# Four PSUM banks instead of two, and a row maximum taken in eight pieces, in the first FFN product of both layers

## The chip, the cores and the metric

The kernel runs on the 8 cores of one Trainium2 chip. Every core runs the same program on one of the 8 batch elements, a 4096 x 1024 float32 array, with its own copy of all weights; the cores exchange nothing. The metric is the device time of the slowest core in microseconds (us). The median of three runs of the kernel before is 11104.93 us.

Each core has five engines that run side by side and wait for each other by semaphores: TensorE (PE in the profile; its weight loads have a row of their own, PEld), VectorE (DVE), ScalarE (ACT), GpSimd (POOL, unused but for constants) and SyncE (SP), which issues all DMAs here.

## The reference

Two layers, each an attention block and an FFN block, each block wrapped in layer norms and a residual. Cut to the part that matters, for one core (`x` is 4096 x 1024):

```
x = x + LN(attn0(LN(x)));   x = x + LN(ffn0(LN(x)))     # layer 0
x = x + LN(attn1(LN(x)));   x = x + LN(ffn1(LN(x)))     # layer 1

act_quant(h):  s = 127 / max(max|h| over the row, 1e-5);  q = clip(round(h*s), -128, 127)
weight_quant:  w -> -1, 0 or 1, with one scale for the whole matrix
ffn:  h = gelu( act_quant(x) @ w1q.T * scales (+ b1 in layer 0) )    # 4096 x 4096
      y = act_quant(h) @ w2q.T * scales (+ b2 in layer 0)
```

Layer 0's FFN has a second layer norm with gamma and beta in front of it and biases b1 and b2; layer 1's has none of these. The quantized numbers are small integers and are held exactly in bf16.

## The kernel before

The kernel is written engine by engine: a function emits a piece of each engine's instruction list, with semaphore waits by hand. Each engine runs its own list strictly in the order in which it was emitted. There is no scheduler. The phases (attention 0, FFN 0, attention 1, FFN 1) are separated by barriers over all engines, and each FFN phase has two halves: the first (product with w1, GELU, quantization, result stored to HBM as `h_q`) and the second (product with w2, layer norm, residual). The change is in the first half, in the function `ffn`.

The first half loops over 32 tiles of 128 rows. For a tile `tt` there are three pieces:

- `front(tt)`: SP loads the rows (`xa`); DVE and ACT take the layer norm's statistics (in layer 0 two norms in a row), DVE the row maximum (L1298) and the scale, ACT scales and rounds (L1352, L1356), DVE clips to bf16 (`xq`, L1316), PE transposes (L181) into `psT`, and DVE copies that to `xqT` (L1322).
- `back_a(tt)`: PE multiplies `xqT` with the 1024 x 4096 weights in eight column groups k of 512; a group is 8 accumulating matmuls (L1395) into one 512-column bank of the PSUM tile `psS` (2048 columns in all). Before, group k uses bank k % 2. In layer 0, DVE scales the group and adds the bias into `ha` (`epi k`, L1411), which frees the bank, and ACT takes the GELU into `hbuf` (`gel k`, L1440). In layer 1, ACT takes the GELU straight from the bank with the scale (`gel k`, L1449), and that frees it. A semaphore mark kept in `ffn1_rel` makes group k wait for the bank's last reader. After `gel7`, DVE takes the maximum of |hbuf| over all 4096 columns in one instruction (L1420), then the scale in four tiny ones (L1423 to L1430) and an empty instruction (L1433) that signals `qn2`; ACT then scales `hbuf` by it (`t2`, L1455; in layer 0 also L1460).
- `back_b(tt)`: DVE clips to bf16 (`hq`; L1479 in layer 0, L1484 and L1488 in layer 1; the mark is `clp2`), and SP stores it.

The loop emits, for k = 0 to 32: `front(k+1)`, `back_b(k-1)`, `back_a(k)`. So on PE the transposes of tile k+1 stand ahead of the groups of tile k, and on DVE everything of `front(k+1)` and the clip of tile k-1 stand ahead of the row maximum of tile k. In layer 1, `gel0` of a tile also waits until the clip of the tile before has read `hbuf` (`hbfree`). The names in the rows drop buffer numbers: `fam` is the row maximum and also, from the change on, its eight partial ones `fam8`; `fst`, `frsc`, `fsact` are [128,1] scales and statistics.

Of the kernel before, what the change touches and what calls it, by code (L numbers as in the profile page):

```python
# [6 lines left out]
F32 = mybir.dt.float32  # L7
BF16 = mybir.dt.bfloat16
AF = mybir.ActivationFunctionType
ALU = mybir.AluOpType  # L10
AX = mybir.AxisListType
# [15 lines left out]
class MK:  # L27
    def __init__(self, phases=("l0a", "l0f", "l1a", "l1f"), debug=False):
# [13 lines left out]
        d = {}  # L42
# [30 lines left out]
        def sb(name, shape, dt, stack=None):  # L73
            return (stack or self._stack).enter_context(nc.sbuf_tensor(name, shape, dt))
# [37 lines left out]
        self.ftmp = sb("ftmp", [128, 32], F32)  # L112
        self.rden = sb("rden", [128, 4], F32)
        self.rden8 = sb("rden8", [128, 8], F32)
        self.am = sb("am", [128, 1], F32)
        self.sact = sb("sact", [128, 1], F32)
        self.rsc1 = sb("rsc1", [128, 1], F32)
# [1053 lines left out]
    def ffn(self, L):  # L1171
        me, blk, d = self, self.block, self.d
# [4 lines left out]
        with contextlib.ExitStack() as ph:  # L1177
            wq1T = self.sb("wq1T%d" % L, [128, 8 * HID], BF16, ph)
            ha = self.sb("ha%d" % L, [128, 4096], F32, ph)
            hb = self.sb("hbuf%d" % L, [128, 4096], F32, ph)  # L1180
# [16 lines left out]
                    self.replicate_vec("bet0", erep, 1024)  # L1197
                self.barrier()

            ffn1_rel = [None, None]  # L1200
            carry = {"xa": [None, None], "trq_prev": None, "gel7_prev": None,
                     "hqst": None}
            plans = {}
# [3 lines left out]
            def seg_marks(P, eng, items):  # L1207
                base = max(me.cnt[eng], _plan[eng])
                mm = {k: base + i + 1 for i, k in enumerate(items)}
                _plan[eng] = base + len(items)  # L1210
                key = {"v": "vm", "s": "sm", "t": "tm"}[eng]
                P.setdefault(key, {}).update(mm)
                return mm

            def buf(tt):
                p = tt % 2
                return dict(
                    lnap=lna[:, p * 1024:p * 1024 + 1024],
                    ln2p=lna[:, 2048:3072],
                    lnxp=lnx[:, 0:1024],  # L1220
                    xqp=xq[:, 0:1024],
                    xqTp=xqT[:, p * 1024:p * 1024 + 1024],
                    st6p=me.fst6[:, p * 12:p * 12 + 12],
                    st2p=me.fst2[:, p * 2:p * 2 + 2],
                    rstdp=me.frstd[:, p:p + 1],
                    nbp=me.fnb[:, p:p + 1],
                    lntp=me.flnt[:, p:p + 1],
                    amp=me.fam[:, p:p + 1],
                    sc1p=me.fsact[:, p * 2:p * 2 + 1],
                    sc2p=me.fsact[:, p * 2 + 1:p * 2 + 2],  # L1230
                    rscp=me.frsc[:, p:p + 1],
                    xap=me.xa[:, p * 1024:p * 1024 + 1024])
# [140 lines left out]
            def back_a(tt):  # L1373
                P, B = plans[tt], buf(tt)
                seg_marks(P, "t", ["mm%d" % k for k in range(8)])
                va = []
                if L == 0:
                    va += ["epi%d" % k for k in range(8)]
                va += ["qn2"]
                seg_marks(P, "v", va)  # L1380
                seg_marks(P, "s", ["gel%d" % k for k in range(8)] +
                          (["t2", "rnd2"] if L == 0 else ["t2"]))
                vm, sm, tm = P["vm"], P["sm"], P["tm"]

                @blk.tensor
                def _(t):
                    for k in range(8):
                        hf = k % 2
                        t.wait_ge(me.semh["v"], vm["evq"])
                        if ffn1_rel[hf] is not None:  # L1390
                            sem, val = ffn1_rel[hf]
                            me.w(t, sem, val)
                        last = None
                        for dc in range(8):
                            last = t.matmul(  # L1395
                                me.psS[:, hf * 512:hf * 512 + 512],
                                B["xqTp"][:, dc * 128:dc * 128 + 128],
                                wq1T[:, dc * HID + k * 512:dc * HID + k * 512 + 512],
                                start=(dc == 0), stop=(dc == 7))
                        assert me.mark(last, "t") == tm["mm%d" % k]  # L1400
                        ffn1_rel[hf] = ("v", vm["epi%d" % k]) if L == 0 else \
                                       ("s", sm["gel%d" % k])

                @blk.vector
                def _(v):
                    if L == 0:
                        for k in range(8):
                            v.wait_ge(me.semh["t"], tm["mm%d" % k])
                            if k == 0 and carry["gel7_prev"] is not None:
                                v.wait_ge(me.semh["s"], carry["gel7_prev"])  # L1410
                            iv = v.scalar_tensor_tensor(  # L1411
                                out=ha[:, k * 512:k * 512 + 512],
                                in0=me.psS[:, (k % 2) * 512:(k % 2) * 512 + 512],
                                scalar=B["rscp"],
                                in1=brep[:, k * 512:k * 512 + 512],
                                op0=ALU.mult, op1=ALU.add)
                            assert me.mark(iv, "v") == vm["epi%d" % k]
                    v.wait_ge(me.semh["s"], sm["gel7"])
                    v.drain()
                    v.tensor_reduce(out=B["amp"], in_=hb[:], axis=AX.X, op=ALU.max,  # L1420
                                    apply_absolute_value=True)
                    v.drain()
                    v.tensor_scalar(out=B["amp"], in0=B["amp"], scalar1=EPS,  # L1423
                                    scalar2=None, op0=ALU.max)
                    v.drain()
                    v.reciprocal(out=B["sc2p"], in_=B["amp"])
                    v.drain()
                    v.tensor_scalar(out=B["sc2p"], in0=B["sc2p"], scalar1=127.0,
                                    scalar2=None, op0=ALU.mult)
                    v.tensor_scalar(out=me.rs2all[:, tt:tt + 1], in0=B["amp"],  # L1430
                                    scalar1=1.0 / 127.0, scalar2=None, op0=ALU.mult)
                    v.drain()
                    assert me.mark(v.nop(), "v") == vm["qn2"]  # L1433

                @blk.scalar
                def _(s):
                    for k in range(8):
                        if L == 0:
                            s.wait_ge(me.semh["v"], vm["epi%d" % k])
                            iv = s.activation(out=hb[:, k * 512:k * 512 + 512],  # L1440
                                              in_=ha[:, k * 512:k * 512 + 512],
                                              func=AF.Gelu)
                        else:
                            s.wait_ge(me.semh["t"], tm["mm%d" % k])
                            if k == 0:
                                s.wait_ge(me.semh["v"], vm["qnt"])
                                if carry.get("hbfree") is not None:
                                    s.wait_ge(me.semh["v"], carry["hbfree"])
                            iv = s.activation(  # L1449
                                out=hb[:, k * 512:k * 512 + 512],  # L1450
                                in_=me.psS[:, (k % 2) * 512:(k % 2) * 512 + 512],
                                func=AF.Gelu, bias=0.0, scale=B["rscp"])
                        assert me.mark(iv, "s") == sm["gel%d" % k]
                    s.wait_ge(me.semh["v"], vm["qn2"])
                    iv = s.activation(out=hb[:], in_=hb[:], func=AF.Identity,  # L1455
                                      bias=me.magic[:], scale=B["sc2p"])
                    assert me.mark(iv, "s") == sm["t2"]
                    if L == 0:
                        s.drain()
                        iv = s.activation(out=hb[:], in_=hb[:], func=AF.Identity,  # L1460
                                          bias=me.nmagic[:], scale=1.0)
                        assert me.mark(iv, "s") == sm["rnd2"]
                carry["gel7_prev"] = sm["gel7"]
# [408 lines left out]
```

## Time and profile before

| what | value |
|---|---|
| median of 3 runs | 11104.93 us (11089.94 to 11122.39) |
| profiled execution | 11115.35 us |
| its span on the slowest core, core 2 | 11113.8 us (fastest core 11079.0) |
| PE / DVE / ACT busy, share of the span | 46% / 40% / 28% |
| DMA queue, share of 16 engines | 13.9% |

No engine is busy for half of the span, so the share of busy time does not say what bounds the kernel; the chain that ended last does. It goes through PE, DVE and ACT by turns (38%, 26% and 18% of the span). A busy PE is not PE at its peak: the granted clock of TensorE (mean 0.70 here) stands in the profile as a share of its full 2.4 GHz, and 0.50 is its lower level, 1.2 GHz.

### The profile page before, as it was taken

How to read it: one execution, taken by the hardware profiler on the slowest of the kernel's cores; microseconds unless marked ns; L12 is line 12 of the kernel's file. 1: busy time of each engine (PE TensorE's matmuls, PEld its weight loads, DVE VectorE, ACT ScalarE, POOL GpSimd, SP SyncE). 2: the span in 40 equal slices, each digit the busy share in tenths (PEclk: the TensorE clock that was granted, in tenths of full speed). 3: DMA queues.
4: the chain of work that ended last, by engine and by line, in shares of the span. 5: the costliest groups of instructions: out<-in, count | busy, mean ns of one | idle time of the engine just before them, and what ended most of it. 6: DMA issues, size and time to landing. Idle time of an engine off the chain costs nothing.

```text
span 11113.8 us, 84236 instructions; the slowest of 8 cores (11079.0 to 11113.8 us)
## 1 busy us (share of the span) xinstructions
PE 5084.5 (46%) x24204; PEld 2302.6 (21%) x24204; DVE 4472.0 (40%) x9414; ACT 3124.4 (28%) x3876; POOL 1.0 (0%) x7
## 2 busy tenths in 40 slices
PE   3445765133333256633333444545544344443666
PEld 1112322111111133311111112212221111111333
DVE  2222333444444432223345555555555433334222
ACT  1111223334444321102223333332332433332111
POOL 0000000000000000000000000000000000000000
PEclk9787777566666668866666666666666577775888
DMA  2111011401111222220000000000001211114222
GB/s 72 42 34 56 29 38 54 146 23 34 34 34 34 98 99 76 76 78 27 27 19 16 16 12 12 8 12 8 8 8 57 89 40 40 40 38 151 76 75 69
DMA packets 159393, 530.32 MB, mean 48 GB/s; under 512 B 49316, under 2 KB 65764, under 8 KB 137447
## 3 DMA queue, kind: packets, MB, share of 16 engines
q1 hardware_dynamic: 158952, 524.93, 13.9%
q8 instruction: 217, 3.56, 0.1%
q14 instruction: 224, 1.84, 0.1%
HBM read 373.88 MB, written 150.99 MB: 47 GB/s over the span
## 4 chain that ended last, share of the span: by engine, by line
PE 38%; DVE 26%; ACT 18%; issue 8%; DMA 4%; DVEq 4%; ACTq 3%; SPq 0%; POOL 0%; POOLq 0%
PE psO L1595 9%; PE psS L1395 8%; PE psT L181 5%; DVE negmh L496 4%; ACT pp L524 4%; PE psS L461 3%; PE psO L1103 3%; PE psO L826 3%; DVE fam L1420 3%; PE psS L654 2%; ACTq L1330 2%; DVE pp L584 2%; DMA wtmp<-w 2%; ACT hbuf L1455 2%; ACT L390 1%
## 5 line engine op out<-in xcount | busy, mean ns | idle before, releaser
L1395 PE MATMUL psS<-wq1T,xqT 128*128 128x512 bf16 x4096 | 1061.7, 426 | 115.4 <-ACT hbuf L1449 100.9
L1595 PE MATMUL psO<-wq2T,hqT 128*128 128x512 bf16 x4096 | 1005.9, 411 | 67.1 <-DVE hqT L1580 67.1
L390 ACT ACT_TABLE_LOAD x128 | 164.2, 1283 | 2891.8 <-DVE st L373 2891.8
L181 PE MATMUL psT<-identb,pp 128*128 128x128 bf16 x4752 | 551.4, 254 | 824.8 <-DVE pp L584 824.4
L496 DVE TENSOR_REDUCE negmh<-psS 128x1 f32<-128x1024 f32 (+5 forms) x720 | 730.1, 1035 | 392.4 <-PE psS L461 369.2
L461 PE MATMUL psS<-kl,qTb 128*128 128x512 bf16 (+3 forms) x1152 | 491.8, 523 | 797.6 <-ACT pp L524 780.1
L524 ACT ACTIVATE pp<-psS,negmh 128x1024 bf16<-128x1024 f32 (+5 forms) x720 | 693.1, 964 | 493.2 <-DVE negmh L496 489.0
L181 PE MATMUL psT<-identb,xq 128*128 128x128 bf16 x512 | 64.7, 307 | 1577.9 <-DVE xq L1316 1577.9
L181 PEld LDWEIGHTS psT<-identb,pp 128*128 128x128 bf16 x4752 | 387.4, 114 | 1054.1 <-issue 935.4
L1395 PEld LDWEIGHTS psS<-wq1T,xqT 128*128 128x128 bf16 x4096 | 440.0, 109 | 712.9 <-issue 343.9
L1121 DVE COPY ppT<-psT 128x512 bf16<-128x512 bf16 x1056 | 443.2, 424 | 347.9 <-PE psT L181 325.1
L1595 PEld LDWEIGHTS psO<-wq2T,hqT 128*128 128x128 bf16 x4096 | 422.9, 104 | 635.5 <-issue 231.7
L1103 PE MATMUL psO<-ppT,vl 128*128 128x512 bf16 x1056 | 463.8, 440 | 196.3 <-DVE ppT L1121 181.0
L1420 DVE TENSOR_REDUCE fam<-hbuf 128x1 f32<-128x4096 f32 x64 | 282.9, 4420 | 507.7 <-ACT hbuf L1449 479.4
L301 ACT ACT_TABLE_LOAD x64 | 82.1, 1283 | 1255.6 <-DVE st L296 1117.2
L181 PE MATMUL psT<-identb,hqs 128*128 128x128 bf16 x2048 | 188.4, 266 | 530.6 <-DVE hqT L1580 515.8
L1610 DVE TENSOR_TENSOR rsc<-rs2all,swv 128x1 f32<-128x1 f32 x64 | 10.2, 160 | 1041.7 <-PE psO L1595 1009.2
L524 ACT ACT_TABLE_LOAD x96 | 123.2, 1283 | 986.9 <-DVE negmh L496 986.9
L181 PE MATMUL psT<-identb,lnb 128*128 128x128 bf16 x512 | 64.8, 307 | 720.0 <-ACT lnb L320 720.0
L181 PEld LDWEIGHTS psT<-identb,xq 128*128 128x128 bf16 x512 | 49.6, 138 | 1608.0 <-issue 1608.0
L461 PE MATMUL psS<-kT,qt 128*128 128x512 bf16 (+3 forms) x1152 | 286.3, 414 | 129.9 <-DVE pp L508 96.9
L1455 ACT ACTIVATE hbuf<-hbuf,magic,fsact 128x4096 f32<-128x4096 f32 x64 | 243.2, 3800 | 355.5 <-DVEq L1433 355.5
(162 smaller groups left out, 7177.6 us busy)
## 6 DMA issues: line engine op xcount, KB each, us to landing
wtmp<-w SPq DMA_DIRECT2D x128, 512.0 KB, 4.2
h_q<-hq SPq DMA_DIRECT2D x64, 1024.0 KB, 4.8
wtmp<-w SPq DMA_DIRECT2D x32, 2048.0 KB, 8.3
hqs<-h_q SPq DMA_DIRECT2D x64, 1024.0 KB, 6.7
xres<-xst SPq DMA_DIRECT2D x96, 512.0 KB, 2.9
xa<-xres SPq DMA_DIRECT2D x96, 512.0 KB, 5.6
xst<-xres SPq DMA_DIRECT2D x96, 512.0 KB, 3.2
xa<-x SPq DMA_DIRECT2D x32, 512.0 KB, 3.6
```

Source lines behind the costliest of these rows:

```text
L181: return te.matmul(out_ap, in_ap, self.identb[:], is_transpose=True, start=start, stop=stop, skip_group_check=True)
L390: s.activation(out=me.lnt[:], in_=me.st2[:, 1:2], func=AF.Ln, bias=me.epsv[:], scale=1.0)
L461: last = t.matmul(ten[:, off + sub:off + sub + sw], qap(dc), kT_ap(dc, CW * c + sub, CW * c + sub + sw), start=(dc == 0), stop=(dc == nchu ...
L496: iv = v.reduce_max(out=me.negmh[:, r * nb + c:r * nb + c + 1], in_=ten[:, off:off + wdt], axis=AX.X, negate=True)
L524: iv = s.activation(out=pp_row[:, CW * c:CW * c + wdt], in_=ten[:, off:off + wdt], func=AF.Exp, bias=me.negmh[:, r * nb + c:r * nb + c + 1 ...
L826: last = t.matmul(me.psO[:, e * 512:e * 512 + 512], ppT[:, ph2 * 512 + jj * 128: ph2 * 512 + jj * 128 + 128], vres[:, jabs * 1024 + e * 51 ...
L1103: iv = t.matmul(me.psO[:, g * 512:g * 512 + 512], vl1[:, (g * NT + j) * 128: (g * NT + j) * 128 + 128], ppT[:, ph2 * 512:ph2 * 512 + 512], ...
L1121: iv = v.tensor_copy(out=ppT[:, ph2 * 512:ph2 * 512 + 512], in_=me.psT[:, ph2 * 1024:ph2 * 1024 + 512])
L1395: last = t.matmul(me.psS[:, hf * 512:hf * 512 + 512], B["xqTp"][:, dc * 128:dc * 128 + 128], wq1T[:, dc * HID + k * 512:dc * HID + k * 512 ...
L1420: v.tensor_reduce(out=B["amp"], in_=hb[:], axis=AX.X, op=ALU.max, apply_absolute_value=True)
L1455: iv = s.activation(out=hb[:], in_=hb[:], func=AF.Identity, bias=me.magic[:], scale=B["sc2p"])
L1595: last = t.matmul(me.psO[:, e * 512:e * 512 + 512], hqT[:, p * 4096 + hc * 128:p * 4096 + hc * 128 + 128], wq2T[:, hc * 1024 + e * 512:hc ...
```

## The change

In `back_a` the eight column groups rotate through four banks of `psS` (k % 4) where they rotated through two, and `ffn1_rel` keeps four marks. The one maximum over 4096 columns becomes eight over 512 columns, each waiting for its own GELU, into the columns of a new [128, 8] tile `fam8`, and a ninth over these eight. The row scale `rs2all` is computed after the drain that stood behind it, and carries the mark `qn2` itself; the empty instruction goes.

```diff
-            ffn1_rel = [None, None]
+            ffn1_rel = [None, None, None, None]
...
-                        hf = k % 2
+                        hf = k % 4
...
-                                in0=me.psS[:, (k % 2) * 512:(k % 2) * 512 + 512],
+                                in0=me.psS[:, (k % 4) * 512:(k % 4) * 512 + 512],
...
-                    v.wait_ge(me.semh["s"], sm["gel7"])
+                    for k in range(8):
+                        v.wait_ge(me.semh["s"], sm["gel%d" % k])
+                        if k == 0:
+                            v.drain()
+                        v.tensor_reduce(out=me.fam8[:, k:k + 1],
+                                        in_=hb[:, k * 512:k * 512 + 512],
+                                        axis=AX.X, op=ALU.max,
+                                        apply_absolute_value=True)
                     v.drain()
-                    v.tensor_reduce(out=B["amp"], in_=hb[:], axis=AX.X, op=ALU.max,
-                                    apply_absolute_value=True)
+                    v.tensor_reduce(out=B["amp"], in_=me.fam8[:], axis=AX.X,
+                                    op=ALU.max, apply_absolute_value=True)
...
-                    v.tensor_scalar(out=me.rs2all[:, tt:tt + 1], in0=B["amp"],
-                                    scalar1=1.0 / 127.0, scalar2=None, op0=ALU.mult)
                     v.drain()
-                    assert me.mark(v.nop(), "v") == vm["qn2"]
+                    iv = v.tensor_scalar(out=me.rs2all[:, tt:tt + 1], in0=B["amp"],
+                                         scalar1=1.0 / 127.0, scalar2=None,
+                                         op0=ALU.mult)
+                    assert me.mark(iv, "v") == vm["qn2"]
...
-                                in_=me.psS[:, (k % 2) * 512:(k % 2) * 512 + 512],
+                                in_=me.psS[:, (k % 4) * 512:(k % 4) * 512 + 512],
```

DVE's list in a middle tile of layer 1 before, from the clip of the tile ahead to the statistics of the tile behind:

```order
L1484 TENSOR_SCALAR hbuf1<-hbuf1,magic 128x4096 [waits s,ev0]
L1488 TENSOR_SCALAR hq1<-hbuf1 128x4096
L1404 UNCONDITIONAL_BRANCH
L1420 TENSOR_REDUCE fam<-hbuf1 128x1 [waits s]
L1423 TENSOR_SCALAR fam<-fam 128x1
L1426 RECIPROCAL fsact<-fam 128x1
L1428 TENSOR_SCALAR fsact<-fsact 128x1
L1430 TENSOR_SCALAR rs2all<-fam 128x1
L1433 NO_OP
L1263 UNCONDITIONAL_BRANCH
L1267 BN_STATS fst6<-xa 128x6 [waits xa0]
```

The same place in the changed kernel, whose lines have moved by one to nine:

```order
L1493 TENSOR_SCALAR hbuf1<-hbuf1,magic 128x4096 [waits s,ev0]
L1497 TENSOR_SCALAR hq1<-hbuf1 128x4096
L1405 UNCONDITIONAL_BRANCH
L1423 TENSOR_REDUCE fam8<-hbuf1 128x1 [waits s] x8
L1428 TENSOR_REDUCE fam<-fam8 128x1
L1431 TENSOR_SCALAR fam<-fam 128x1
L1434 RECIPROCAL fsact<-fam 128x1
L1436 TENSOR_SCALAR fsact<-fsact 128x1
L1439 TENSOR_SCALAR rs2all<-fam 128x1
L1264 UNCONDITIONAL_BRANCH
L1268 BN_STATS fst6<-xa 128x6 [waits xa0]
```

One waiting reduction has become eight that wait (`x8`) and one that does not; the empty instruction is gone. What stands ahead and behind is the same. On PE and ACT the lists keep their instructions and their order; only the banks and the values waited for change.

## Rows read from the trace of the kernel before

**Rows 1.** The page: chain that ended last, shares by engine and line.
```profile
PE psO L1595 9%; PE psS L1395 8%; PE psT L181 5%; DVE negmh L496 4%; ACT pp L524 4%; PE psS L461 3%; PE psO L1103 3%; PE psO L826 3%; DVE fam L1420 3%; PE psS L654 2%; ACTq L1330 2%; DVE pp L584 2%; DMA wtmp<-w 2%; ACT hbuf L1455 2%; ACT L390 1%
```

**Rows 2.** The same chain in 9390 to 9440 us, layer 1, by line.
```profile
by line: PE psS L1395 26.2%; DVE fam L1420 17.7%; ACTq L1330 13.7%; issue 8.0%; ACT hbuf L1455 6.4%; DVE hbuf L1484 4.7%; DVE hq L1488 4.6%; ACT hbuf L1449 4.2%; ACT lna L1335 2.5%; ACT lnx L1352 2.5%; DVE fam L1298 2.4%; ACT lnx L1356 2.3%
```

**Rows 3.** Groups, layer 0 (2300 to 3800): busy us, mean ns | idle before, releaser.
```profile
L1395 PE MATMUL psS<-wq1T,xqT 128*128 128x512 bf16 x2048 | 519.7, 421 | 14.5 <-DVE ha L1411 14.5
...
L1420 DVE TENSOR_REDUCE fam<-hbuf 128x1 f32<-128x4096 f32 x32 | 141.4, 4420 | 28.3 <-ACT hbuf L1440 28.3
```

**Rows 4.** The same groups in layer 1 (8770 to 10040).
```profile
L1395 PE MATMUL psS<-wq1T,xqT 128*128 128x512 bf16 x2048 | 542.0, 431 | 100.9 <-ACT hbuf L1449 100.9
...
L1420 DVE TENSOR_REDUCE fam<-hbuf 128x1 f32<-128x4096 f32 x32 | 141.4, 4420 | 479.4 <-ACT hbuf L1449 479.4
```

**Rows 5.** Timeline of one tile, layer 1: start, duration, what [idle before].
```profile
9396.69 0.15 DVE L1428 TENSOR_SCALAR fsact<-fsact 128x1 f32<-128x1 f32 x1
...
9397.08 3.80 ACT L1455 ACTIVATE hbuf<-hbuf,magic,fsact 128x4096 f32<-128x4096 f32 x1 [5.50 <-DVEq L1433]
...
9411.01 4.62 PE L1395 MATMUL psS<-wq1T,xqT 128*128 128x512 bf16 x16
...
9417.45 0.32 SPq L1257 DMA_DIRECT2D xa<-xres  x1
9418.27 1.27 ACT L1449 ACTIVATE hbuf<-psS,frsc 128x512 f32<-128x512 f32 x2
...
9419.10 12.21 PE L1395 MATMUL psS<-wq1T,xqT 128*128 128x512 bf16 x48 [3.48 <-ACT hbuf L1449]
...
9429.68 0.69 ACT L1449 ACTIVATE hbuf<-psS,frsc 128x512 f32<-128x512 f32 x1 [1.04 <-PE psS L1395]
9431.41 0.69 ACT L1449 ACTIVATE hbuf<-psS,frsc 128x512 f32<-128x512 f32 x1 [1.04 <-PE psS L1395]
9432.25 4.42 DVE L1420 TENSOR_REDUCE fam<-hbuf 128x1 f32<-128x4096 f32 x1 [15.35 <-ACT hbuf L1449]
```

**Rows 6.** Stretches of that tile, line L1395: PE and PEld busy, PEclk.
```profile
9411.00:9413.00 2.00, 1.99 (x5) 0.77 (x6) 0.50 0.00 0
...
9416.00:9419.00 3.00, 0.00 (x0) 0.00 (x0) 1.00 0.42 175
9419.20:9422.00 2.80, 2.80 (x9) 1.05 (x9) 0.62 0.93 272
```

**Rows 7.** Timeline of PE, another tile of layer 1.
```profile
8889.27 6.06 PE L1395 MATMUL psS<-wq1T,xqT 128*128 128x512 bf16 x16
8897.37 12.21 PE L1395 MATMUL psS<-wq1T,xqT 128*128 128x512 bf16 x48 [2.04 <-ACT hbuf L1449]
```

**Rows 8.** Timeline of PE, the last tile of layer 1.
```profile
10015.10 13.22 PE L1395 MATMUL psS<-wq1T,xqT 128*128 128x512 bf16 x48 [13.79 <-ACT hbuf L1449]
```

**Rows 9.** Timeline of one tile, layer 0: two statistics, then the row maximum.
```profile
2905.55 0.69 DVE L1267 BATCH_NORM_STATS2 fst<-xa 128x6 f32<-128x512 f32 x1 [0.29 <-issue]
2906.16 0.68 DVE L1268 BATCH_NORM_STATS2 fst<-xa 128x6 f32<-128x512 f32 x1
...
2946.21 0.75 DVE L1411 SCALAR_TENSOR_TENSOR ha<-psS,frsc,brep 128x512 f32<-128x512 f32 x1 [0.97 <-PE psS L1395]
2947.06 0.63 ACT L1440 ACTIVATE hbuf<-ha 128x512 f32<-128x512 f32 x1 [1.09 <-DVE ha L1411]
2947.84 4.42 DVE L1420 TENSOR_REDUCE fam<-hbuf 128x1 f32<-128x4096 f32 x1 [0.88 <-ACT hbuf L1440]
2952.34 0.15 DVE L1423 TENSOR_SCALAR fam<-fam 128x1 f32<-128x1 f32 x1
```

**Rows 10.** Groups of DVE, all phases: the small reductions.
```profile
L496 DVE TENSOR_REDUCE negmh<-psS 128x1 f32<-128x512 f32 x36 | 24.9, 691 | 9.8 <-PE psS L461 7.4
...
L537 DVE TENSOR_REDUCE negM<-negmh 128x1 f32<-128x4 f32 x72 | 6.8, 150 | 18.7 <-ACT pp L524 17.4 <-DVE pp L508 1.3
```

**Rows 11.** The load of the FFN's rows (L1257): issue to landing.
```profile
DMA to landing us min/median/max: 3.1/5.6/6.4
```

More of the change, by code:

```diff
@@ L114, in __init__ @@
         self.rden8 = sb("rden8", [128, 8], F32)
+        self.fam8 = sb("fam8", [128, 8], F32)
         self.am = sb("am", [128, 1], F32)
```

## The prediction

> **What bounds the kernel now.** I read the chain of waits first, since no engine is busy for half of the span. Over the whole program the first FFN product (L1395) has 8% of it and the row maximum behind the GELU (L1420) 3% [rows 1]. Cut out for one stretch of layer 1's first FFN half the picture is sharper: the product has 26.2%, the maximum 17.7%, and the rest is a single thread that changes engine at each step [rows 2]. So in layer 1 nothing overlaps the chain: what is cut from a link comes off the end.
>
> Next, the groups by stage. In layer 0 PE runs its 2048 matmuls in 519.7 us and waits only 14.5 us, in one piece; DVE waits 28.3 us in 32 pieces, 0.88 us each, ahead of its maximum. In layer 1 PE is busy 542.0 us and waits another 100.9 us for the GELU's banks, and DVE sits idle 479.4 us ahead of the maximum, about 15 us a tile [rows 3, 4].
>
> The timeline of one tile shows why [rows 5]. PE starts at 9411.01, fills two banks in 4.62 us and stops. The first GELU can start only at 9418.27, behind the clip of the tile before. It frees a bank, and PE goes on at 9419.10, 8.09 us after its start; in a tile whose first two groups took 6.06 us it was 8.10 [rows 7]. Six groups take 12.21 us more, the last GELU starts at 9431.41 and the 4.42 us maximum at 9432.25. The clock shows what the stop costs beyond itself: 0.50 at the start of the stream, 1.00 in the stop, and 0.62 in the first 2.8 us behind it [rows 6], so that PE pays for two slow starts. At 1.00 a group takes 1.73 us (the distance of the last two GELUs, which each wait for PE [rows 5]), or 0.216 us a matmul; at 0.50 twice that.
>
> **The change part by part.**
>
> *A, the tail of the maximum, layer 1.* Before, the large reduction starts 0.84 us after the last GELU starts, and the next DVE instruction follows 4.50 us later (2947.84 to 2952.34 [rows 9]). After, seven of the eight pieces fit in the time in which DVE was idle: GELUs come 0.63 us apart at the tightest (1.27 us for two) and 1.73 us apart towards the end [rows 5]. Only the last piece is behind the last GELU. A 512-column reduction takes 0.69 us and one of 4 columns 0.15 us [rows 10]; the first was from PSUM, but statistics over 512 columns of SBUF also take 0.69 [rows 9]. With 0.08 us from an end to a dependent start (2952.26 to 2952.34 [rows 9]) that is 0.69 + 0.08 + 0.15 + 0.08 = 1.00 us. Gain 3.50 us a tile.
>
> *B, the row scale before the signal, both layers.* Before, the scale's instruction at 9396.69 and ACT's start at 9397.08 are 0.39 us apart, with `rs2all` nearly beside the former [rows 5]. After, it comes behind it: 0.15 + 0.08 + 0.14, then 0.10 us from a marked DVE end to ACT's start (2946.96 to 2947.06 [rows 9]), 0.47 us. Loss 0.08 us a tile. ACT waits for exactly this, so nothing hides it. A and B together: 3.42 x 32 tiles = 109.4 us off layer 1.
>
> *C, four banks, layer 1.* Before, the stream takes busy plus wait: 542.0 + 100.9 = 642.9 us. The last tile has no transposes in front of it and a stream of its own, 13.79 + 13.22 us and 3.5 us of two groups at full clock [rows 8], 30.5 us. The other 31 take 612.4 / 31 = 19.75 us each. After, the third and fourth groups run in the old stop. The fifth needs the first GELU's bank, free at 8.09 us as before. How long the first four take hangs on when the clock rises. The mean stop of the other 31 tiles is (100.9 - 13.79) / 31 = 2.8 us, so their first two groups take 8.09 - 2.8 = 5.2 to 5.3 us; four take 5.2 + 2 x 1.73 = 8.7 us, beyond 8.09, so that the bank is free. The whole stream is 5.2 + 6 x 1.73 = 15.6 us. Gain 19.75 - 15.6 = 4.15 us a tile, x 31 = 128.7 us. Bounds: where the first two groups take 4.62 us [rows 5], the fifth starts at about 8.09 and the stream is 8.1 + 4 x 1.73 = 15.0 us, gain 147 us; where they take 6.06 us [rows 7] it is 16.4 us, gain 103 us. Layer 0's unbroken streams average 519.7 / 32 = 16.2 us [rows 3], inside these bounds. I take the middle, because layer 1's own first groups give it.
>
> *D, the last tile of each half.* There PE waits long with two groups done (13.79 us [rows 8], 14.5 us in layer 0 [rows 3]). With four done, two groups leave the end: 2 x 1.73 = 3.5 us in each layer, 7.0 us.
>
> *E, the pieces in layer 0.* Here all eight pieces stand behind the last bias instruction on DVE, so none of them is hidden behind another engine's work except the last GELU's 0.88 us wait. The last bias instruction ends at 2946.96; a drained start follows 0.09 later; the pieces follow each other as two independent statistics of the same size do, 0.61 us from start to start [rows 9]: 0.09 + 7 x 0.61 + 0.69 + 0.08 + 0.15 + 0.08 = 5.36 us to the next tiny instruction, against 5.38 before. With B's 0.08 that is 0.06 us x 32 = 1.9 us lost. Bounds: nothing to gain below that pace; at most each piece pays its 0.69 us and a fresh 0.15 us wait (9432.10 to 9432.25 [rows 5]), 0.84 apart: 7 x 0.23 = 1.6 us a tile more, 54 us in all. I take the low end, since only the pair is the same case: independent, same engine, nothing late. The banks do nothing in layer 0: PE never waited for one except in D.
>
> The Trainium skill (VectorE: DVE Perf Modes, section The DRAIN you can't avoid) says that after a Vector instruction "the next op does not start until the 8-stage pipe empties". By that the pieces would be 0.69 apart, layer 0 would lose 18 us more and the sum would come to 10880; the trace does not agree, as the second statistic starts 0.08 us before the first ends.
>
> *Covers.* The new rows' load is issued at 9417.45 and lands at most 6.4 us later [rows 11], 9423.9. Their statistics move from behind 9432.25 + 5 us to about 9429.5, so 5 us of cover are left. PE's idle time between streams shrinks by the tail's 3.4 us; I give nothing for a warmer start, as a 13.79 us wait did not keep the clock up either (48 matmuls in 13.22 us where full clock needs 10.4 [rows 8]).
>
> *Sum.* -109.4 (A, B) - 128.7 (C) - 7.0 (D) + 1.9 (E) = -243.2 us on 11115.35, the profiled execution: 10872. The median of the runs is 10.4 us lower; the same cut on it gives 10862. The other cores, at most 35 us shorter, run the same chain.
>
> **The rivals.**
>
> *1. The pieces cost their full price in layer 0.* For it: eight waits and eight starts a tile on DVE's path. Against: the pair 0.61 apart. Price 54 instead of 1.9 us: -191, 10914.
>
> *2. The stream gains nothing.* The clock could fall again in mid-stream as it does now, or PE could stop at the fifth group for as long as now at the third. For it: the fifth still waits for the same GELU. Against: four groups outlast 8.09 us on average. Then only A, B and E count: -107.5, 10997.
>
> *3. Slower: the clock never rises in layer 1's stream.* If writing four banks by turns kept the granted clock at 0.50 throughout, a stream takes 64 x 0.432 = 27.6 us, 7.9 more than now, x 31 = 245, against 107.5 gained: +137, 11242. The point from which it decides is a stream longer than 19.75 + 3.4 = 23.2 us. Against: layer 0's unbroken streams take 16.2 us [rows 3], so the clock rises in them, with the same matmuls and a bank change every group.
>
> The Trainium skill (TensorE: Matmul & The Clock Gate, section A second HAM failure mode: psum-queue depth-cycling) describes matmuls of this size that cycle through PSUM banks and idle briefly between groups until the clock swings between its levels. By it the outcome would lie between rivals 2 and 3; layer 0's rows, which also change bank each group, speak against it.
>
> *4. It does nothing that can be measured*, because a wait I have not seen (the load, the store of `hq`) takes the place of the stop: 11105. Against: the 5 us of cover above.
>
> **How the numbers follow.** Forecast 0.80, rival 1 0.09, rival 2 0.06, rival 3 0.03, rival 4 0.02. The bounds of C put the forecast's own range at 10843 to 10888, and run to run the kernel before spreads over 32 us. Rival 1 has 0.09, so I reach just past it: 10838 to 10916. A measurement of this kernel tells about 0.3% (33 us) from no change; the forecast and rivals 1 and 2 lie beyond that: faster 0.95, same 0.02, slower 0.03.
>
> **What would show it.** In layer 1: PE's wait for the GELU down from 100.9 to some 10 us, all but a few in the last tile; streams of 15 to 16.4 us; the last piece starting 0.84 us behind the last GELU and the next tiny instruction 1.00 us behind that; tiles about 7.6 us closer together. In layer 0: pieces 0.61 us apart and tiles as far apart as before. I am wrong if PE stops at the fifth group for more than a microsecond in most tiles, if the clock is at 0.50 for over a third of a stream, or if the pieces start 0.7 us or more apart.

## The result and the profile after

The changed kernel takes 10873.73 us, median of 8 runs, against 11115.45 us of the kernel before, 8 runs beside it: ratio 0.9784, 95% interval 0.9769 to 0.9799. That is 241.7 us less; 243.2 were forecast. The profiled execution took 10869.97 us with a span of 10867.6 on its slowest core, core 7.

The two groups of layer 1 that answer to [rows 4], and the small reduction (columns: busy us, mean ns | idle before, releaser):

```profile
L1396 PE MATMUL psS<-wq1T,xqT 128*128 128x512 bf16 x2048 | 499.7, 408 | 7.7 <-ACT hbuf L1458 6.9
...
L1423 DVE TENSOR_REDUCE fam<-hbuf 128x1 f32<-128x512 f32 x256 | 167.9, 683 | 200.5 <-ACT hbuf L1458 200.1 <-issue 0.2
...
L1428 DVE TENSOR_REDUCE fam<-fam 128x1 f32<-128x8 f32 x32 | 5.2, 161 | 2.4
```

PE's wait for a bank is down from 100.9 to 6.9 us, and that is one piece, in the last tile. Its busy time is down as well, by 42 us with the same 2048 matmuls: the second slow starts are gone. DVE's waits are now between the pieces, where the GELUs set the pace. In layer 0 the stream is what it was in [rows 3], but for the wait in the last tile (11.4 us for 14.5):

```profile
L1396 PE MATMUL psS<-wq1T,xqT 128*128 128x512 bf16 x2048 | 519.4, 421 | 11.4 <-DVE ha L1412 11.4
```

A tile of layer 1, the counterpart of [rows 5] (timeline: start, duration, what [idle before]):

```profile
9523.66 15.16 PE L1396 MATMUL psS<-wq1T,xqT 128*128 128x512 bf16 x64
...
9530.10 0.32 SPq L1258 DMA_DIRECT2D xa<-xres  x1
9530.93 2.43 ACT L1458 ACTIVATE hbuf<-psS,frsc 128x512 f32<-128x512 f32 x4
9531.77 2.46 DVE L1423 TENSOR_REDUCE fam<-hbuf 128x1 f32<-128x512 f32 x4 [2.21 <-ACT hbuf L1458]
...
9538.92 0.69 ACT L1458 ACTIVATE hbuf<-psS,frsc 128x512 f32<-128x512 f32 x1 [1.04 <-PE psS L1396]
9539.72 0.69 DVE L1423 TENSOR_REDUCE fam<-hbuf 128x1 f32<-128x512 f32 x1 [1.04 <-ACT hbuf L1458]
9540.48 0.16 DVE L1428 TENSOR_REDUCE fam<-fam 128x1 f32<-128x8 f32 x1
9540.72 0.15 DVE L1431 TENSOR_SCALAR fam<-fam 128x1 f32<-128x1 f32 x1
...
9541.41 0.15 DVE L1439 TENSOR_SCALAR rs2all<-fam 128x1 f32<-128x1 f32 x1
9541.66 0.69 DVE L1268 BATCH_NORM_STATS2 fst<-xa 128x6 f32<-128x512 f32 x1
9541.66 3.80 ACT L1464 ACTIVATE hbuf<-hbuf,magic,fsact 128x4096 f32<-128x4096 f32 x1 [2.05 <-DVE rs2all L1439]
```

The 64 matmuls are one unbroken row. The first GELU still starts 7.27 us behind the stream's start, as in [rows 5], but by then four groups are done and four GELUs run in a row. The last piece starts 0.80 us behind the last GELU, and the next tiny instruction 1.00 us behind that. The load issued at 9530.10 has 11.6 us until its statistics.

The clock in the same tile (stretch; PE and PEld busy; PEclk) rises once and stays. So it does in 30 of layer 1's tiles on each of the 8 cores (the last two follow each other without a break): it rises 1.5 to 5.2 us into the stream and falls in none.

```profile
9523.00:9525.00 2.00, 1.34 (x4) 0.60 (x5) 0.50 0.03 8
9526.00:9530.00 4.00, 4.00 (x20) 1.82 (x19) 1.00 0.00 0
9530.00:9538.60 8.60, 8.57 (x40) 3.65 (x38) 1.00 0.53 183
```

The end of a tile of layer 0, beside [rows 9]:

```profile
2970.26 0.75 DVE L1412 SCALAR_TENSOR_TENSOR ha<-psS,frsc,brep 128x512 f32<-128x512 f32 x1 [0.97 <-PE psS L1396]
2971.11 4.84 DVE L1423 TENSOR_REDUCE fam<-hbuf 128x1 f32<-128x512 f32 x8
2976.02 0.16 DVE L1428 TENSOR_REDUCE fam<-fam 128x1 f32<-128x8 f32 x1
2976.25 0.15 DVE L1431 TENSOR_SCALAR fam<-fam 128x1 f32<-128x1 f32 x1
```

Eight pieces with a wait each take 4.84 us, and the next tiny instruction starts 5.24 us behind the end of the last bias instruction (2971.01), against 5.38 before. Nothing is gained that matters, and nothing lost: layer 0's tiles are 47.7 to 47.8 us apart, as before, while layer 1's went from 40.0 us to 32.6.

### The profile page after: what moved, and what is told of

Its sections match the earlier page's. It is cut to its first block, busy times and chain, and to the rows that moved or that the text cites. A ratio compares the mean times of both kernels' runs of the same rounds, so it can differ in the third digit from the quotient of the medians.

```text
span 10867.6 us, 85192 instructions; the slowest of 8 cores (10829.9 to 10867.6 us)
## 1 busy us (share of the span) xinstructions
PE 5024.7 (46%) x24204; PEld 2281.8 (21%) x24204; DVE 4528.6 (42%) x9926; ACT 3124.1 (29%) x3876; POOL 1.0 (0%) x7
## 4 chain that ended last, share of the span: by engine, by line
PE 39%; DVE 24%; ACT 17%; issue 8%; DVEq 4%; DMA 4%; ACTq 3%; SPq 0%; POOL 0%; POOLq 0%
PE psO L1604 9%; PE psS L1396 9%; PE psT L182 5%; DVE negmh L497 4%; ACT pp L525 4%; PE psS L462 3%; PE psO L1104 3%; PE psO L827 3%; PE psS L655 2%; ACTq L1331 2%; DVE pp L585 2%; DMA wtmp<-w 2%; ACT hbuf L1464 2%; DVE ppT L1122 2%; ACT L391 1%
## 5 line engine op out<-in xcount | busy, mean ns | idle before, releaser
L1604 PE MATMUL psO<-wq2T,hqT 128*128 128x512 bf16 x4096 | 1028.8, 418 | 67.5 <-DVE hqT L1589 67.5
L1396 PE MATMUL psS<-wq1T,xqT 128*128 128x512 bf16 x4096 | 1019.1, 415 | 19.0 <-DVE ha L1412 11.4
L1423 DVE TENSOR_REDUCE fam<-hbuf 128x1 f32<-128x512 f32 x512 | 322.7, 680 | 203.4 <-ACT hbuf L1458 200.1
L462 PEld LDWEIGHTS psS<-kl,qTb 128*128 128x128 bf16 x1152 | 89.8, 103 | 1184.2 <-issue 1162.5
```

The costliest lines, as they stand in the source:

```text
L462: last = t.matmul(ten[:, off + sub:off + sub + sw], qap(dc), kT_ap(dc, CW * c + sub, CW * c + sub + sw), start=(dc == 0), stop=(dc == nchu ...
L1396: last = t.matmul(me.psS[:, hf * 512:hf * 512 + 512], B["xqTp"][:, dc * 128:dc * 128 + 128], wq1T[:, dc * HID + k * 512:dc * HID + k * 512 ...
L1423: v.tensor_reduce(out=me.fam8[:, k:k + 1], in_=hb[:, k * 512:k * 512 + 512], axis=AX.X, op=ALU.max, apply_absolute_value=True)
L1604: last = t.matmul(me.psO[:, e * 512:e * 512 + 512], hqT[:, p * 4096 + hc * 128:p * 4096 + hc * 128 + 128], wq2T[:, hc * 1024 + e * 512:hc ...
```

## The experiments

The theory: layer 1's chain loses the stop with the slow start behind it (C), and seven eighths of the maximum (A); the two add up, and layer 0 is left alone. Rivals: the parts need each other; a stop costs what it does because of the clock, whatever its length; the pieces cost layer 0 their price.

**Banks alone.** The kernel before with `k % 4` and four marks, nothing else.

> The kernel before with the four banks alone; the one large maximum and the old signal stay. Theory (the banks are worth what the product's stream loses in its stop and its second slow start, terms C and D): layer 1's streams 15.5 to 15.7 us on average, PE's wait for the GELU in layer 1 down from 100.9 to about 10 us, 136 us off the kernel before. Rival (the stream is shortened only together with the pieces, since the maximum sets when the next tile starts and with that when the clock rises): anything from 110 to 154 us, with streams of 15.0 or of 16.4 us in nearly every tile. Second rival (the stop moves to the fifth group): under 30 us.

Ratio 0.9877 (0.9832 to 0.9923), 137 us off, 86 to 187 by the interval, so the time alone decides nothing between the theory and the first rival. Layer 1 on core 1:

```profile
L1395 PE MATMUL psS<-wq1T,xqT 128*128 128x512 bf16 x2048 | 502.6, 410 | 11.1 <-ACT hbuf L1449 10.7
...
L1420 DVE TENSOR_REDUCE fam<-hbuf 128x1 f32<-128x4096 f32 x32 | 141.4, 4420 | 350.3 <-ACT hbuf L1449 350.3
```

The whole of C is there without the pieces: 513.7 us busy and waiting, where the kernel before had 642.9. The second rival (the stop moves to the fifth group) falls. The first, that the parts need each other, falls by the streams: they last from 15.2 to 16.5 us on this core and 15.7 on average, as in the whole change, and not 15.0 or 16.4 in nearly every tile.

**Pieces alone.** Two banks, eight pieces, the old signal.

```diff
-                    v.wait_ge(me.semh["s"], sm["gel7"])
+                    for k in range(8):
+                        v.wait_ge(me.semh["s"], sm["gel%d" % k])
...
                     v.drain()
-                    v.tensor_reduce(out=B["amp"], in_=hb[:], ...
+                    v.tensor_reduce(out=B["amp"], in_=me.fam8[:], ...
```

> The kernel before with the eight pieces of the maximum alone; two banks and the old signal stay. Theory (term A without B, and E): 3.50 us a tile of layer 1, nothing in layer 0 (0.02 us a tile less): 112 to 113 us off the kernel before, the next tiny instruction 1.00 us behind the last piece's start, tiles of layer 0 at 47.7 to 47.8 us. Rival (every piece waits for the one ahead to end, 0.69 us or more apart): layer 0's tiles 0.6 us longer, 95 us off. With the first run of this call it tests the sum: both together and 5 us for the signal should give the whole change's 242 us.

Ratio 0.9896 (0.9871 to 0.9922), 116 us off. The stop is untouched, in layer 1 on core 6:

```profile
L1396 PE MATMUL psS<-wq1T,xqT 128*128 128x512 bf16 x2048 | 542.6, 432 | 98.6 <-ACT hbuf L1457 98.6
```

So A is worth its own time on the chain and no more. The two parts and the signal's 5 us make 137 + 116 - 5 = 248 us; the whole change has 240 by its ratio, well inside the intervals. The distance of layer 1's tiles (mean of a core's 30, median of the cores) tells it more closely: 40.0 us before, 36.1 with the banks alone, 36.4 with the pieces alone, 32.6 with both, so that 3.9 and 3.6 us apart stand against 7.4 together. Layer 0's tiles are 47.7 to 47.8 us apart in this run as in the kernel before, which removes the rival on the pieces.

**Three banks.** `k % 3` in the changed kernel.

> The changed kernel with three banks instead of four. The fourth group then waits for the first GELU's bank, 8.1 us after the stream's start; three groups take 6.7 to 7.0 us on average, so a stop of about 1.2 us comes back (0.4 to 2.0). Theory (a stop costs its length, and a second slow start only when it is long): layer 1's streams 16.7 us, 36 us more in layer 1 and 3.5 us more in the two last tiles than the changed kernel, 40 us in all. Rival (any stop brings the second slow start that most tiles had before, 1.7 us in 22 of 30): 75 us more than the changed kernel, streams of 18 to 18.5 us.

Ratio 0.9833 (0.9796 to 0.9870), 0.5% or some 54 us above the whole change's; the intervals overlap, and 54 lies between the theory's 40 and the rival's 75, so the times do not decide. Two tiles of layer 1, PE:

```profile
9101.86 8.79 PE L1396 MATMUL psS<-wq1T,xqT 128*128 128x512 bf16 x40 [0.93 <-ACT hbuf L1458]
...
9127.42 7.40 PE L1396 MATMUL psS<-wq1T,xqT 128*128 128x512 bf16 x24
9135.52 8.79 PE L1396 MATMUL psS<-wq1T,xqT 128*128 128x512 bf16 x40 [0.70 <-ACT hbuf L1458]
```

Behind a stop of 0.93 or 0.70 us the 40 matmuls take 8.79 us; at full clock they need 8.64. So no second slow start, while the six groups behind the stops of 3.48 and 2.04 us in [rows 5, 7] took 12.21 us instead of 10.4. The streams are 16.89 us (9127.42 to 9144.31) in nearly every tile, where 16.7 were expected: the stop costs its length, and the fourth bank takes it away. Layer 1's tiles are 33.7 us apart, 1.2 us more than in the changed kernel, or 37 us over 32 tiles, where 36 were expected. On all eight cores the stop was at most 1.8 us, the last tile aside, and the clock fell behind none.

The other half of the theory, that a stop brings a second slow start when it is long, is not shown. In the kernel before, the clock stayed up behind some longer stops too:

```profile
9500.77 12.21 PE L1395 MATMUL psS<-wq1T,xqT 128*128 128x512 bf16 x48 [3.35 <-ACT hbuf L1449]
...
9541.29 10.52 PE L1395 MATMUL psS<-wq1T,xqT 128*128 128x512 bf16 x48 [3.13 <-ACT hbuf L1449]
```

Of that core's 30 tiles between the first and the last, the six groups of 8, behind stops of 1.9 to 3.2 us, took 10.52 us; in 22, behind stops of 2.0 to 3.8 us, the clock fell. And the stop with three banks comes behind 24 matmuls, not behind 16. What decides it is open.

**The signal.** In the changed kernel the scale's instruction carries the mark and `rs2all` follows.

```diff
-                    v.drain()
-                    iv = v.tensor_scalar(out=me.rs2all[:, tt:tt + 1], in0=B["amp"],
+                    iv = v.tensor_scalar(out=B["sc2p"], in0=B["sc2p"], scalar1=127.0,
...
+                    v.tensor_scalar(out=me.rs2all[:, tt:tt + 1], in0=B["amp"],
```

> The changed kernel, with the signal for ScalarE carried by the scale's own instruction and the row scale for the second half computed behind it. Theory (term B: ScalarE waits for exactly this signal): from the tiny instruction behind the maximum to the start of ScalarE's scaling 0.23 us less than in the changed kernel, 0.15 us less than before, 14 to 15 us off the changed kernel over 64 tiles. Rival (something else is as late as the signal, or the next statistics on VectorE come later and are waited for): no difference beyond 3 us.

Ratio 0.9761 (0.9737 to 0.9785): the times can't tell it from the whole change (medians 10883.74 and 10873.73 us). The waits can (engine line <- releaser: us in total, times, longest). First the changed kernel, then this one, in layer 1:

```profile
ACT hbuf L1464 <- DVE rs2all L1439: 68.8, 32, 2.7
```
```profile
ACT hbuf L1463 <- DVE fsact L1436: 60.3, 32, 2.1
```

8.5 us less over 32 tiles, 0.27 us a tile. The mechanism holds. That 14 us come off the end is not shown by the times, though the two profiled executions point to it: layer 1's tiles are 32.4 us apart instead of 32.6, layer 0's 47.3 instead of 47.8 (means of a core's 30, median of the cores), and the median of cores 0 to 3, at the same mean clock of 0.707, ends at 10815 us instead of 10835.

**Four pieces of 1024.**

> The changed kernel with four pieces of 1024 columns instead of eight of 512. Theory (behind the last GELU stands one piece and what it costs is its length; in layer 0 each piece costs its columns and some 0.06 us): layer 1's tail 1.22 + 0.31 = 1.53 us instead of 1.00, 17 us more over 32 tiles; layer 0's reductions 0.2 to 0.3 us a tile shorter, 6 to 10 us less; in all 7 to 11 us slower than the changed kernel, which the times cannot tell from none and the trace can. Rival (pieces of 512 cost a start of their own): layer 0 1 us a tile shorter, faster in all by 15 us.

Ratio 0.9779 (0.9748 to 0.9811), no different. The end of a tile, in layer 1 and in layer 0:

```profile
9247.07 1.22 DVE L1423 TENSOR_REDUCE fam<-hbuf 128x1 f32<-128x1024 f32 x1 [2.23 <-ACT hbuf L1458]
...
9248.60 0.15 DVE L1431 TENSOR_SCALAR fam<-fam 128x1 f32<-128x1 f32 x1
...
2969.87 4.60 DVE L1423 TENSOR_REDUCE fam<-hbuf 128x1 f32<-128x1024 f32 x4
```

The tail in layer 1 is 1.53 us instead of 1.00; layer 0's pieces take 4.60 us instead of 4.84. Both sizes are as the theory has them, so a piece costs its columns and 0.06 us. The rival, 1 us a tile less in layer 0, falls. The tiles moved further than these rows do: layer 1's are 33.4 us apart (32.6 with eight pieces), layer 0's 47.1 to 47.5 (47.7 to 47.8); the rest lies in the lengths of the streams, and why they differ is open.

**Groups ahead of the transposes.** The rows show PE idle for 16 us ahead of each tile's transposes, with groups behind them that need nothing of it. With the early signal, six banks (two of `psO`), and the PE list in another order:

```diff
             for k in range(NT + 1):
+                if k < NT:
+                    groups(k, range(6))
                 if k + 1 < NT:
                     plans[k + 1] = {}
                     front(k + 1)
...
+                for k in range(8):
+                    if k == 6:
+                        groups(tt, (6, 7))
```

> The kernel with the early signal and six banks (two more from the PSUM tile of the second product), in which the first six groups of a tile stand on TensorE ahead of the next tile's transposes instead of behind them: they need only the copy of the tile before, so they can run while VectorE and ScalarE work on scale, norm and rounding. Theory (what is left of the stream in the chain is the groups behind the first freed bank): two groups instead of four behind it, 6.8 us at the lower clock, as TensorE has then been idle for long. Layer 0: last bias instruction about 5.2 us earlier, 160 us. Layer 1: from the first GELU to the last 7.8 us instead of 8.5, 22 us. With 7 us in the last tiles 190 us off the kernel with the early signal alone, some 445 us off the kernel before. Rival (the groups ahead hold up the transposes, or the clock has fallen so that nothing is won): layer 0 under 2 us a tile, layer 1 slower than now, in all under 60 us.

10570.03 us, ratio 0.9507 (0.9480 to 0.9535): about 548 us off the kernel before, 100 more than expected. The mechanism is as told, but the last two groups were priced too high. In layer 1, and in layer 0:

```profile
8990.41 2.43 ACT L1471 ACTIVATE hbuf<-psS,frsc 128x512 f32<-128x512 f32 x4
8991.25 12.87 PE L1394 MATMUL psS<-wq1T,xqT 128*128 128x512 bf16 x48 [7.89 <-ACT hbuf L1471]
...
8997.31 0.69 ACT L1471 ACTIVATE hbuf<-psS,frsc 128x512 f32<-128x512 f32 x1 [1.70 <-PE psS L1394]
...
9012.95 1.01 PE L182 MATMUL psT<-identb,xq 128*128 128x128 bf16 x8 [5.39 <-DVE xq L1317]
```
```profile
2943.75 12.42 PE L1394 MATMUL psS<-wq1T,xqT 128*128 128x512 bf16 x48 [3.87 <-DVE ha L1426]
...
2949.37 0.75 DVE L1426 SCALAR_TENSOR_TENSOR ha<-psS,frsc,brep 128x512 f32<-128x512 f32 x1 [1.19 <-PE psS L1394]
```

From the freed bank to the last GELU it is 6.06 us, where 6.8 were expected, and in layer 0 5.62 us to the last bias instruction: the clock rises inside these 16 matmuls. That makes some 60 of the 100 us over 32 tiles of each layer; where the rest comes from is open. PE waits 5.39 us for the next transposes' input, so the groups ahead do not hold them up, and the rival falls. Layer 0's tiles are 40.9 us apart (47.8 before), layer 1's 30.3 (32.6 in the changed kernel). And PE waits 7.89 us a tile for the first GELU, which waits for the clip.

**The clip in front.** The same, with the clip of tile k - 1 placed in `front(k + 1)` (the comments are added here):

```diff
-                    v_items = ["bn1", "nb1"]
+                    v_items = ["bn1", "nb1", "clp2q"]      # layer 1; bn1, clp2q, nb1 in layer 0
...
+                    if Q is not None:
+                        clip_1(v, Q)     # layer 0: the clip; layer 1: its first instruction
                     v.wait_ge(me.semh["s"], sm["st1"])
...
+                    if Q is not None:
+                        clip_2(v, Q)     # layer 1: its second instruction
```

> The kernel with groups ahead, and the clip of the tile before moved on VectorE from behind the next tile's transposed copy to the front of that tile's work, where VectorE waits for ScalarE: in layer 0 ahead of the norm's first bias, in layer 1 one of its two instructions ahead of it and one behind it. Theory (in layer 1 the first GELU waits for this clip and nothing else): layer 1's tiles from about 31.6 to 25 to 26 us, 180 us; layer 0's 1.8 us shorter, 54 us; some 235 us off the kernel with groups ahead alone, 10430 to 10460 us in all. Rival (the clip now holds up the norm of the next tile by as much as it releases the GELU): layer 1 within 1 us a tile of the kernel with groups ahead.

10318.56 us, ratio 0.9279 (0.9253 to 0.9306): 251 us off the kernel with groups ahead, where 235 were expected, and 5% under the changed kernel. The 10430 to 10460 us expected in all were undercut, mostly because the groups ahead had already given 100 us more than the sum allowed them. Layer 1's tiles are 23.8 us apart, layer 0's 39.2.

```profile
8849.45 2.35 DVE L1246 TENSOR_SCALAR hbuf<-hbuf,magic 128x4096 f32<-128x4096 f32 x1 [2.35 <-ACT hbuf L1512]
...
8851.72 0.15 DVE L1306 SCALAR_TENSOR_TENSOR fnb<-fst,frstd 128x1 f32<-128x1 f32 x1
8851.97 2.29 DVE L1256 TENSOR_SCALAR hq<-hbuf 128x4096 bf16<-128x4096 f32 x1
...
8858.81 1.28 ACT L1506 ACT_TABLE_LOAD   x1
8858.97 0.69 DVE L1352 TENSOR_SCALAR xq<-lnx 128x1024 bf16<-128x1024 f32 x1 [2.82 <-ACT lnx L1392]
8859.92 1.01 PE L182 MATMUL psT<-identb,xq 128*128 128x128 bf16 x8 [6.67 <-DVE xq L1352]
8860.11 2.42 ACT L1506 ACTIVATE hbuf<-psS,frsc 128x512 f32<-128x512 f32 x4
```

The first GELU no longer waits for anything but ScalarE's own list: it starts 0.19 us behind the transposes' start, where it came 8.1 us behind. The rival, that the clip holds up the norm as much, falls: layer 1's tiles are 6.5 us closer than with groups ahead alone.

## Why the prediction was right

The mechanism came out as told, term by term. That the total agrees within 1.5 us is luck: the interval on the ratio is 17 us wide to either side, and two small terms were off.

*A*: 1.00 us from the last piece to the next tiny instruction was forecast and measured; the gain is 3.50 us a tile. The pieces alone gave 116 us where 112 to 113 were expected.

*B*: from the first tiny instruction to ScalarE's start it is 0.94 us (9540.72 to 9541.66), and was 0.85 in a tile before. 0.08 was forecast.

*C*: the stream was to be 15.0 to 16.4 us and 15.6 on average; it is 15.2 to 16.6 us on the profiled core, 15.65 on average. Busy and waiting, layer 1's stream lost 642.9 - 507.4 = 135.5 us; C and layer 1's half of D had 132, and the other 3.4 are the last tile's shorter tail, which A counts already. Experiment by experiment: a bank less gives its stop back, and the banks alone give all of C. Tiles of layer 1 were to be 7.6 us closer together, and are 7.4.

*D*: the last tile's wait is 6.9 us where it was 13.79, 3.5 from two more groups and 3.4 from the shorter tail, as D and A have it. In layer 0 it fell by 3.1 us (14.5 to 11.4) where 3.5 were forecast.

*E*: forecast a loss of 1.9 us in layer 0. The pieces are 0.59 us apart, not 0.61, and the tail is 5.24 us, not 5.36, 0.12 us a tile less. Over 32 tiles the term is 3.8 us too high, so that layer 0 gains some 2 us instead of losing 1.9, which no time can show. The Trainium skill's sentence on the pipe (VectorE: DVE Perf Modes, The DRAIN you can't avoid), taken alone as the prediction took it, does not hold for these independent reductions: eight of about 0.68 us each take 4.84. The same section says that a next op that is not held starts earlier, and these rows agree with that.

*The rivals.* 1 falls by layer 0's rows, 2 by the unbroken stream, 3 by the clock, at 1.00 from 2.3 us on in the stream shown and from 5.2 us at the latest in any, 4 by the load's 11.6 us. The swing of the clock between groups that the Trainium skill tells of (TensorE: Matmul & The Clock Gate, A second HAM failure mode: psum-queue depth-cycling) does not show with four banks by turns: the clock falls in none of the 240 streams of layer 1 counted above. The kernel before shows something near it, a fall to 0.50 behind the one stop of a stream.

What the prediction left out is what the last two experiments found: it took the order of the lists as given, and said of the first GELU only that it starts when the clip is done.

## What to carry to other kernels

Where one thread changes engine at each step, what is cut from a link comes off the end, and the gain can be added up link by link: here each term came out within some 4 us. Cut a reduction so that only its last piece stands behind the last producer, and give a matmul stream as many banks as it fills before the first reader can start. Then ask of each instruction in the chain whether it needs the one ahead of it in its list: here two moved pieces, with two more banks, gave more than twice what the banks and pieces did.

## What the runs showed of the hardware

Stops of TensorE of 0.2 to 1.8 us behind 24 matmuls left the granted clock at full speed in all 232 tiles counted in the run with three banks (29 on each of 8 cores). In the kernel before, stops of 1.9 to 3.9 us behind 16 matmuls were followed by a fall to 0.50 in 151 of 232 tiles, the shortest of 1.95 us, and by none in 81, the longest of 3.18 us: the length of the stop alone did not decide it. Eight independent reductions of 512 columns with a satisfied wait before each run at 0.59 us a piece, with 0.68 us shown for one. And streams of layer 1 in the changed kernel mostly alternate between 15.2 us and 15.8 to 16.4 us from tile to tile, as the clock rises earlier or later in them; why they alternate is open.
